# Context attention of a perceiver stack: TensorE's and ScalarE's programs for the first three double batches written out instead of looped

## The reference

```python
keys   = ctx * cos + rotate_half(ctx) * sin          # rotary, per batch, 1601 x 128
scores = q_latent @ keys.T                           # 64 tokens x 16 heads per batch
p      = exp(scores - max(scores))
context = (p / sum(p)) @ keys                        # 128 channels per token and head
```

## Time and profile before

| | us |
|---|---|
| median of three runs (1365.62 to 1365.66) | 1365.63 |
| the profiled execution | 1364.51 |
| its span, first to last instruction | 1362.7 |
| TensorE busy (97% of the span) | 1321.3 |
| VectorE busy (69%) | 938.6 |
| GpSimd busy (49%) | 661.1 |
| ScalarE busy (46%) | 624.0 |
| TensorE's three loop passes begin at about | 541, 646, 755 |
| the last double batch begins at about | 863 |

### The profile page before, as it was taken

One profiled execution on the slowest core, in us unless ns is written; L12 is line 12 of the kernel. 1 busy time (PEld: TensorE's weight loads), 2 busy tenths in 40 slices (PEclk: granted clock), 3 DMA queues, 4 the chain that ended last, 5 costly groups with the idle time before them and its releaser, 6 DMA issues.

```text
span 1362.7 us, 22745 instructions
## 1 busy us (share of the span) xinstructions
PE 1321.3 (97%) x8567; PEld 1085.0 (80%) x8567; DVE 938.6 (69%) x1427; ACT 624.0 (46%) x1293; POOL 661.1 (49%) x478
## 2 busy tenths in 40 slices
PE   8999999999999998999999899999999999999998
PEld 5777778778875665999899899999878888767886
DVE  5556766659658996877677687877446777565555
ACT  3524443253333335666566566666324546631000
POOL 3342577768736867044043141400464656635663
PEclk9999999999999999999999899999999999999999
DMA  4121223323342220000000001000231222212321
GB/s 151 49 78 49 62 83 95 88 76 93 93 167 72 71 61 26 26 1 27 1 26 26 2 26 38 20 1 1 74 111 47 79 78 64 92 47 85 99 94 62
DMA packets 31187, 83.20 MB, mean 61 GB/s; under 512 B 3440, under 2 KB 5616, under 8 KB 30704
## 3 DMA queue, kind: packets, MB, share of 16 engines
q1 hardware_dynamic: 31088, 81.81, 19.3%
HBM read 80.75 MB, written 1.05 MB: 60 GB/s over the span
## 4 chain that ended last, share of the span: by engine, by line
PE 89%; DVE 4%; ACT 3%; issue 2%; POOL 1%; DMA 0%; ACTq 0%; POOLq 0%; DVEq 0%
PE psum L925 24%; PE psum L927 23%; PE psum L926 23%; PE psum L1477 6%; PE psum L953 1%; PE psum L1411 1%; PE psum L995 1%; PE psum L1424 1%; PE psum L1000 1%; PE psum L996 1%; PE psum L1373 1%; PE psum L964 1%; PE psum L1680 1%; DVE xc L2264 1%; PE psum L1654 1%
## 5 line engine op out<-in xcount | busy, mean ns | idle before, releaser
L671 POOL TENSOR_SCALAR wpair<-landing 128x1024 fp32r<-128x1024 f32 (+3 forms) x115 | 104.2, 906 | 369.8 <-PE psum L927 212.0
L674 POOL TENSOR_TENSOR wpair<-landing,wpair 128x1024 fp32r<-128x1024 f32 (+3 forms) x115 | 220.5, 1917 | 9.6
L925 PE MATMUL psum<-xn,wpair 128*128 128x512 f32 x548 | 222.8, 407 | 0.4 <-POOL wpair L674 0.4
L926 PE MATMUL psum<-xn,wpair 128*128 128x512 f32 x548 | 216.2, 395 | 0.0
L927 PE MATMUL psum<-xn,wpair 128*128 128x512 f32 x548 | 215.9, 394 | 0.0
L2257 DVE TENSOR_TENSOR expo_t<-psum,expo_t 128x512 fp32r<-128x512 f32 (+1 forms) x224 | 144.1, 650 | 76.1 <-ACT expo_t L2040 72.7
L2040 ACT CAST expo_t<-psum 128x512 fp32r<-128x512 f32 (+1 forms) x224 | 124.2, 565 | 130.3 <-PE psum L1477 130.3
L925 PE MATMUL psum<-expo_t,kv_pair 128*128 128x256 f32 (+1 forms) x416 | 134.1, 322 | 0.2 <-DVE expo_t L2257 0.2
L2685 DVE TENSOR_REDUCE part_max<-psum 128x1 f32<-128x804 f32 x126 | 120.5, 986 | 12.2 <-PE psum L927 10.1
L1477 PE MATMUL psum<-const,expo 128*128 128x128 f32 (+1 forms) x832 | 127.4, 273 | 0.9 <-DVE expo_t L2257 0.6
L925 PEld LDWEIGHTS psum<-xn,wpair 128*128 128x128 f32 x548 | 103.3, 188 | 30.8 <-issue 7.0
(11 more groups left out here) (324 smaller groups left out, 3058.7 us busy)
## 6 DMA issues: line engine op xcount, KB each, us to landing
landing<-in_weights SPq DMA_DIRECT2D x60, 512.0 KB, 3.5
landing<-in_weights SPq DMA_DIRECT2D x103, 256.0 KB, 2.6
kv<-in_ctx SPq DMA_DIRECT2D x8, 832.0 KB, 4.8
landing<-in_weights SPq DMA_DIRECT2D x15, 320.0 KB, 2.8
landing<-in_weights SPq DMA_DIRECT2D x16, 192.0 KB, 2.3
rotary_w<-in_rotary SPq DMA_DIRECT2D x1, 1920.0 KB, 10.0
rope_k<-in_rope_k SPq DMA_DIRECT2D x1, 1664.0 KB, 13.9
const<-in_constants SPq DMA_DIRECT2D x1, 1184.0 KB, 8.6
```

What stands on the lines that cost most here:

```text
L671: pool.tensor_scalar(wpair[:, slot, 0, 0:width], landing[:, slot, 0:width], 1.0, 1.0, ALU.mult, ALU.mult).then_inc(chunk_high, 1)
L674: pool.tensor_tensor(wpair[:, slot, 1, 0:width], landing[:, slot, 0:width], wpair[:, slot, 0, 0:width].bitcast(F32), ALU.subtract).then_in ...
L925: pe.matmul(out, w(0), act(0), start=start, stop=False)
L926: pe.matmul(out, w(0), act(1), start=False, stop=False)
```

## The change

In TensorE's and in ScalarE's program the hardware loop over i becomes a Python loop, so that the eight units are written into the program three times, with constants where registers were. Nothing else is changed: VectorE's, GpSimd's and SP's programs are the same instruction for instruction.

```diff
--- before.py
+++ after.py
@@ -1568,7 +1568,7 @@
                 score_row(0, 1, 0)
                 for q in range(3):
                     turn_exp(0, 0, q, TURN_BANKS[q])
-                with pe.Fori(0, B // 2 - 1) as i:
+                for i in range(B // 2 - 1):
                     units(i, False)
                 units(B // 2 - 1, True)
 
@@ -2104,7 +2104,7 @@
                         exps(0, unit, r, step)
                 for q in range(3):
                     exp_t_in(0, 0, q, TURN_BANKS[q])
-                with act.Fori(0, B // 2 - 1) as i:
+                for i in range(B // 2 - 1):
                     units(i, False)
                 units(B // 2 - 1, True)
```

## The result

| | before | after |
|---|---|---|
| median, first comparison (4 runs each) | 1365.62 us | 1348.26 us |
| its ratio, 95% interval | | 0.9881 (0.9866 to 0.9896) |
| median, second comparison (13 and 4 runs) | 1361.19 us | 1348.31 us |
| its ratio, 95% interval | | 0.9910 (0.9893 to 0.9926) |
| the profiled execution, first comparison | 1364.51 us | 1348.21 us |

The change made the kernel faster by 17.4 us in the first comparison, where 12.0 us were forecast and 8.6 to 14.3 us were in the range. In the second comparison, with more runs of the kernel before, it won 12.9 us by the medians; its interval means 10.1 to 14.6 us.

A forecast was written before the change was run, and what follows sets the result against it. TensorE, busy 97% of the span, was taken to bound the kernel. Its two back branches (11.51 us) plus the unit behind the second crossing (0.53) gave 12.04 us, so 1365.63 became 1353.6 us, range 1351.3 to 1357.0.

The forecast's parts named there:

- The crossings: L1492-to-L1492 distances containing a pass's end on TensorE; the two that branch back, 18.10 and 18.25 us, should become 12.4.
- the exit's 12.42: Third L1492 distance over a pass's end, where TensorE's branch falls through into the last double batch: 12.42 us.
- The forecast's two terms: TensorE's two back branches go, each pass end shrinking to 12.42 us: 5.68 and 5.83 us, together 11.51 us.
- The unit behind the second crossing: Unit after the second pass's end, stretched by slow clock to 13.38 us against 12.85 behind the exit; 0.53 us won.
- The bracket that named ScalarE: Profile puts 1.50 us of TensorE's wait before L925 down to ScalarE's exponential L2033; the prediction blamed TensorE's branch.
- rival 1: ScalarE's wait before L925 is real: its 1.50 us stay, only 4.9 us of issue go, 1360.7 us; chance 5%.
- the straight code: TensorE's written-out bodies, fetched in a straight line: cost nothing; 0.67 us for each of some 18 packets would cancel the gain.
- stretch of half clock: TensorE's clock at half speed after idle times; none expected between 541 and 950 us, later ones 1.7 us each.
- rival 3: Longer program shifts L1600 and L1777 against packet borders; L1600's five back branches cost 28.5 us, time 1382.1; chance 3%.
- its own spread: The forecast's range, 1351.3 to 1357.0 us: later half-clock stretches come or go, 1.7 us each; the first crossing's unit may gain.
- The sequencer fetches the block with the branch's target and then the block behind it: At TensorE's back branch: a reading of 2 packets of 16 KB moved around the third matmul's 2.69 us issue wait.
- Rival 2: TensorE's long branch hides something waited for anyway; gain only the branches' own 83 ns, three times: 1365.4 us; chance 4%.

The follow-up runs named there:

- experiment 2: Kernel before with only TensorE's loop written out, ScalarE keeping its loop: 1348.47 us, ratio 0.9908 to the kernel before.
- experiment 3: Kernel before with only ScalarE's loop written out, TensorE keeping its loop: 1362.54 us, ratio 1.0015 to the kernel before.
- experiment 1: The kernel before again, with no edit: 1361.93 us in 12 runs, ratio 1.0003 to the kernel before.
- experiment 5: The changed kernel again, with no edit, beside the kernel before on the same chip: 1348.31 us against 1361.19, ratio 0.9910.
- experiment 4: Kernel before, both loops kept, with ten already satisfied waits put in front of TensorE's loop: 1348.12 us, ratio 0.9914 to the kernel before.

## Why the prediction was wrong in size and right in kind

**Right.** The crossings were the place: 18.10 and 18.25 us became 12.28 and 12.31 us, where the exit's 12.42 had been taken as the price. The forecast's two terms, 5.68 and 5.83 us, measured 5.82 and 5.94. The unit behind the second crossing gave 0.54 us where 0.53 were forecast. The bracket that named ScalarE was false (rival 1 falls, experiments 2 and 3), ScalarE's loop gave nothing, the straight code waits for issue nowhere, and no new stretch of half clock came in its place. The later loops L1600 and L1777 keep branches of 0.2 us:

```profile
L1600 PEldq COMPARE_BRANCH  x6: 76/208/238, 952.9 to 987.9; - x6
...
L1777 PEldq COMPARE_BRANCH  x3: 76/208/209, 1261.9 to 1329.1; - x3
```

so rival 3 did not come to pass.

**Wrong: the sum was made against runs of the kernel before that start late, and the range left the start out.** The step that failed is "its own spread", with the 1365.63 us that the sum starts from: it let later stretches of half clock come and go by 1.7 us each and took everything ahead of the loop as fixed, since the same code runs there. The kernel before was 2.67 us late there in its profile against the changed kernel, behind weights that landed late (412.77 us, where they were there at 410.18 in experiment 1), and stood another 1.1 us above that in its median. Three runs within 0.04 us looked like a kernel without spread; 57 more of the same kernel reach from 1357.2 to 1366.9 us. Against the medians of these (1361.2 to 1362.7 us) the changed kernel wins 12.9 to 14.4 us; the comparison made on one chip gives 12.9, close to the 12.0 forecast. What put the other runs of the first comparison at 1365.6 us stays open.

**Wrong by a little: 1.5 us in the loop.** The loop itself gave 13.55 us where 12.04 were forecast. 0.25 of it are the two crossings. The largest other piece is the unit that ran from 801.03 to 814.11 in the third pass, 13.08 us, against 12.27 in the profile after: VectorE's `q_pair` low part took 2.15 us there, with GpSimd at work on `kv` beside it (2.40 us from 803.50), and 0.91 us in the changed kernel. I had seen that row and given it no term. It is not the change's gain either: in experiment 1, the same kernel again, this unit takes 12.27 us, and the loop as a whole is then 12.56 us longer than the changed kernel's in experiment 5.

```profile
804.02 2.15 DVE L2257 TENSOR_TENSOR q_pair<-big,q_pair 128x256 fp32r<-128x256 f32 x1
```

and its like in the profile after:

```profile
788.77 0.91 DVE L2257 TENSOR_TENSOR q_pair<-big,q_pair 128x256 fp32r<-128x256 f32 x1
```

**The cause was told only in part.** "The sequencer fetches the block with the branch's target and then the block behind it" is what happens at the branch. But the prediction took it that going back far always costs this. Experiment 4 shows that it doesn't: the same branch to the same distance costs 0.2 us with five instructions more in front. Rival 2 was built on a page of the Trainium skill (Runtime: NRT & Kernel Launch, Instruction fetch mechanics) that gives TensorE room for 2048 instructions, in which this body would fit. I set the page aside because of the packets. The runs agree with that size as far as a body of 1,820 instructions stays. It doesn't settle the matter, since bodies of 1,652 and 1,876 instructions are fetched anew. The same section says that only two blocks are held; by that the branch of experiment 4 would have to fetch, and it doesn't, so for TensorE the measurement decides against it.

## What to carry to other kernels

When a long hardware loop pays microseconds at its branch, look whether instruction packets come in every pass and at which matmul the wait for issue stands. If the body is near what the engine can hold, shifting its start by a few instructions can win what writing it out wins, and any edit ahead of the loop can lose it again. Before a small gain is priced, learn how far the kernel before spreads over more than three runs; and use a crossing that falls through as the measure for one that doesn't, which here held to 0.15 us.

## What the runs showed of the hardware that I had not expected

- TensorE's branch back over 1,652 instructions takes 3.3 to 4.0 us or 0.2 us, by the place of the body alone.
- Two waits of a program become one instruction of 51 ns: 10 waits are 5, 240 are 120. These start 0.11 us apart (120 between 536.9 and 549.9 us), and TensorE stands behind them: 11.3 us of waiting for issue with 240.
- TensorE's granted clock falls to half at 22 us in some profiles and not in others, though the code there is the same. Its lag of 1.5 us is gone by the loop: the first L1492 is at 541.42 and 541.85 us with it (experiments 1 and 3), at 541.38 and 542.04 without (experiments 4 and 5). What did reach the loop was one late landing of weights.
